# Waits of a fused attention and mixture kernel, set at other points

## The reference

```python
def attn(data, weight, mask):                       # 32x32 block mask
    block_mask = mask.reshape(nb, 32, kb, 32).sum(axis=(1, 3)) > 0
    elem_mask = repeat(repeat(block_mask, 32, 0), 32, 1)
    return einsum('bsk,nk->bsn', data, weight * elem_mask)

def ffn(x, W_base, b_base, W_router, A, B):         # 8 experts, rank 16, top 2
    probs = softmax(x @ W_router.T); combine = normalised top-2 weights
    h = einsum('nd,erd->ner', x, A)
    expert_out = einsum('ner,eor->no', h * combine[:, :, None], B) * 2.0
    return x @ W_base.T + b_base + expert_out

x = x + attn(layernorm(x), weight, mask)            # x: (2, 4096, 4096) float32
x = x + ffn(layernorm(x), W_base, b_base, W_router, A, B)
```

## Time and profile before

| | |
|---|---|
| median of 3 runs | 1446.66 us (1446.52 to 1446.85) |
| profiled execution | 1448.56 us |
| its span, slowest core | 1446.9 us |
| spans of the cores | 1428.7 to 1446.9 us |
| PE busy | 1012.2 us (70%) |
| DVE busy | 518.3 us (36%) |
| moved by DMA | 179.69 MB |

### The profile page before, as it was taken

The page is one execution under the profiler, slowest core; times in us unless marked ns, Lnnn a source line. Parts: engine busy times, 40 slices in busy tenths (PEclk is TensorE's granted clock), DMA queues, the critical chain, the costliest instruction groups (busy, mean ns, idle before and its releaser), DMA issues.

```text
span 1446.9 us, 19848 instructions; the slowest of 8 cores (1428.7 to 1446.9 us)
## 1 busy us (share of the span) xinstructions
PE 1012.2 (70%) x8874; PEld 854.6 (59%) x8874; DVE 518.3 (36%) x656; ACT 9.7 (1%) x26; POOL 32.2 (2%) x48
## 2 busy tenths in 40 slices
PE   0000000002599999999999806499999999999997
PEld 0000000000488888888888703388888888888886
DVE  2446888662435455445536143400001000000010
ACT  0000000000000000000000000000000000000000
POOL 0000000000000000000000000000000000000000
PEclk9999999999999999999999957699999999999999
DMA  8999989961533533533443089434444555544441
GB/s 207 270 260 236 298 250 285 287 230 28 91 59 71 106 59 60 100 76 59 81 96 60 9 163 162 75 72 104 88 88 88 98 110 117 114 88 88 88 95 53
DMA packets 107887, 179.69 MB, mean 124 GB/s; under 512 B 68234, under 2 KB 84762, under 8 KB 103706
## 3 DMA queue, kind: packets, MB, share of 16 engines
q0 software_dynamic: 19792, 77.67, 30.0%
q1 hardware_dynamic: 85578, 67.17, 17.0%
q10 hardware_dynamic: 2432, 33.57, 6.7%
HBM read 222.48 MB, written 16.78 MB: 165 GB/s over the span
## 4 chain that ended last, share of the span: by engine, by line
PE 67%; DMA 17%; DVE 10%; SPq 4%; issue 2%; DVEq 0%; ACT 0%; POOL 0%; POOLq 0%; ACTq 0%
PE pp L620 32%; PE pp L380 31%; DMA xres<-x_in 10%; DVE ost L220 4%; SPq L148 4%; DMA wts<-mask_in 3%; PE pp L635 2%; DMA packed<-bmt_sb 2%; PE pp L629 2%; DVE scr L251 2%; DMA wts<-wta 1%; DVE wts L335 1%; DMA xnt<-ost 1%; DMA r<-bp_l 1%; DVE bnall L413 0%
## 5 line engine op out<-in xcount | busy, mean ns | idle before, releaser
L380 PE MATMUL pp<-wts,xnt 128*128 128x256 bf16 x4096 | 448.9, 273 | 26.5 <-DVE wts L335 26.5
L620 PE MATMUL pp<-wts,xnt 128*128 128x256 bf16 x4096 | 460.9, 276 | 0.0
L380 PEld LDWEIGHTS pp<-wts,xnt 128*128 128x128 bf16 x4096 | 401.5, 98 | 73.8 <-issue 26.7
L620 PEld LDWEIGHTS pp<-wts,xnt 128*128 128x128 bf16 x4096 | 405.0, 99 | 53.7 <-issue 0.4
L232 PE MATMUL pp<-ost,bd_sb 128*4 128x128 bf16 x32 | 8.5, 265 | 291.8 <-DVE ost L220 291.8
L651 DVE TENSOR_TENSOR ost<-pp,xres 128x256 f32<-128x256 f32 x128 | 43.9, 416 | 469.0 <-PE pp L635 469.0
L335 DVE TENSOR_TENSOR wts<-wts,r 128x8192 bf16<-128x8192 bf16 x16 | 139.1, 8693 | 159.1 <-DMA wts<-wta 159.1
L232 PEld LDWEIGHTS pp<-ost,bd_sb 128*4 128x4 bf16 x32 | 2.6, 80 | 293.7 <-issue 293.7
L220 DVE TENSOR_REDUCE ost<-wts 128x128 bf16<-128x4096 int32 x32 | 141.4, 4420 | 90.3 <-DMA wts<-mask_in 87.1
L348 DVE TENSOR_TENSOR xres<-pp,xres 128x256 bf16<-128x256 f32 x128 | 43.9, 415 | 101.2 <-PE pp L380 101.2
L465 PE MATMUL pp<-wrt,xnt 128*128 128x8 bf16 x256 | 7.7, 167 | 48.9 <-DMA xnt<-xstg 35.0
(11 more groups left out here) (51 smaller groups left out, 133.3 us busy)
## 6 DMA issues: line engine op xcount, KB each, us to landing
wts<-mask_in ACTq DMA_DIRECT2D x16, 2048.0 KB, 10.3
wts<-mask_in SPq DMA_DIRECT2D x16, 2048.0 KB, 11.3
wts<-wta POOLq DMA_DIRECT2D x16, 2048.0 KB, 14.7
wts<-wtb POOLq DMA_DIRECT2D x16, 2048.0 KB, 16.8
y_out<-ost SPq DMA_DIRECT2D x16, 1024.0 KB, 16.1
xres<-x_in POOLq DMA_DIRECT2D x8, 1024.0 KB, 19.7
r<-at_l POOLq DMA_DIRECT2D x1, 1024.0 KB, 7.9
r<-bp_l POOLq DMA_DIRECT2D x1, 1024.0 KB, 7.8
```

The costliest lines, as they stand in the source:

```text
L380: f = (lambda t, kt=kt, tt=tt, b=b, bank=bank, c0=c0, st=st: t.matmul(bank[:, c0:c0 + slab_n], xnt[:, tt, kt, :], wts[:, b, kt, :], start= ...
L620: top(lambda t, kt=kt, tt=tt, b=b, bank=bank: t.matmul(bank[:, 256 * (tt % 2):256 * (tt % 2) + slab_n], xnt[:, tt, kt, :], wts[:, b, kt, : ...
```

## The change

The first transpose of the first layer norm no longer waits for the loads of all x tiles. The weight loads of attention's slabs 0 and 1 wait for the last mask reduction that reads the buffer in question, where all loads waited for the whole mask and all transposes; the multiplication by the mask (slabs 0 and 1) waits for the mask, and the first matmul for the transposes. The loads of at, bp and bias wait only for the last multiplication by the mask, and no longer for each other; the first transpose of the second layer norm does not wait for them.

```diff
--- before.py
+++ after.py
@@ -257,8 +257,6 @@
             if i >= 13 and (i - 13) % 2 == 0 and (i - 13) // 2 < n_tt:
                 tt = (i - 13) // 2
                 w = [(pV, ln1_ap[tt])]
-                if tt == 0:
-                    w.append((sXc, c_xcast_all))
                 ln1_xb[tt] = xbar((sB0 if tt % 2 == 0 else sB1),
                                   xnt[:, tt, :, :], ln1_src(tt), waits=w)
             if i >= 11 and (i - 11) % 2 == 0 and (i - 11) // 2 < n_tt:
@@ -330,7 +328,9 @@
         def emit_attn_apply(s):
             b = s % 2
             w = [((sW0 if b == 0 else sW1), c_wcast[s])]
-            if s >= 2:
+            if s < 2:
+                w.append((pV, v_mask_done))
+            else:
                 w.append((pT, t_slab[s - 2]))
             return vop(lambda v, b=b, s=s: v.tensor_tensor(
                 wts[:, b].rearrange("p a (j r) -> p a j r", r=32),
@@ -356,11 +356,12 @@
         v_applies = []
         for s in range(n_slab):
             b = s % 2
-            w = [(sB0, ln1_b0), (sB1, ln1_b1), (pV, v_mask_done)]
-            if debug and s < 2:
-                w.append((sAt, dbg_pre_attn))
-            if s >= 2:
-                w.append((pT, t_slab[s - 2]))
+            if s < 2:
+                w = [(pV, v_red[n_mtile - 2 + s])]
+                if debug:
+                    w.append((sAt, dbg_pre_attn))
+            else:
+                w = [(pT, t_slab[s - 2])]
             c_wcast.append(dma(RG, (sW0 if b == 0 else sW1),
                                wts[:, b, :, :].rearrange("p a c -> p (a c)"),
                                wta[s], waits=w, max_dma_last_dim=8192))
@@ -368,6 +369,9 @@
             if s >= 1:
                 pass
             w = [(pV, v_applies[s])]
+            if s == 0:
+                w.append((sB0, ln1_b0))
+                w.append((sB1, ln1_b1))
             if s >= 2:
                 w.append((pV, v_evac[s - 2]))
             first = True
@@ -441,12 +445,9 @@
         ln2_aggr = [None] * n_tt
 
         c_at = dma(RG, sAt, at3.rearrange("p a c -> p (a c)"), at_l[:],
-                   waits=[(pT, t_attn_done), (pV, v_applies[-1])],
-                   max_dma_last_dim=8192)
-        c_bp = dma(RG, sAt, bprime, bp_l[:], waits=[(sAt, c_at)],
-                   max_dma_last_dim=8192)
-        c_bias = dma(RG, sAt, bias_sb[:, :], bias_in,
-                     waits=[(pV, v_mask_done), (sAt, c_bp)])
+                   waits=[(pV, v_applies[-1])], max_dma_last_dim=8192)
+        c_bp = dma(RG, sAt, bprime, bp_l[:], max_dma_last_dim=8192)
+        c_bias = dma(RG, sAt, bias_sb[:, :], bias_in)
 
         tw = min(4, n_tt)
         nth = n_tt // tw
@@ -522,8 +523,6 @@
                 xstg_ln2[pb], xres[:, tt, :], ri_buf[pb][:], nm_buf[pb][:],
                 op0=ALU.mult, op1=ALU.add), waits=wap)
             w = [(pV, ln2_ap[tt]), (pT, t_attn_done)]
-            if tt == 0:
-                w.append((sAt, c_bias))
             ln2_xb[tt] = xbar((sB0 if tt % 2 == 0 else sB1),
                               xnt[:, tt, :, :], xstg_ln2[tt % 2], waits=w)
             emit_router(tt)
```

## The result

The changed kernel takes 0.9862 of the time before (95% interval 0.9832 to 0.9892), about 20 us less; its profiled execution took 1428.27 us, its span is 1426.7 us, and the undisturbed runs lie between 1427.85 and 1430.58 us. The forecast was 1430.5. That ratio has a condition on which much of this study turned: it leaves out the runs in which single cores were far behind, and of the changed kernel's first ten timed runs those are five, with 1455 to 1474 us. The median of all ten is 1442.94 us, against 1447.04 us before. Runs in which the cores of one die were held back together at a lower granted clock (1494 to 1654 us, the kernel before among them) are in no count in this document.

The account below looks back on a forecast made before the run. The slowest core, core 3, was taken to set the time, with gains only outside its unbroken matmul stages; 0 + 7.6 + 8.5 = 16.1 us off 1448.56 gives 1432.4, less 1.9 to the runs' median: 1430.5 us, range 1421 to 1441.

Parts of the forecast that it names:

- part 1: First layer norm: first transpose no longer waits for all x; 0 to 1.9 us on core 3, taken as 1.
- part 2: Before attention: weight loads 0 and 1 go out early; 17.3 us less 9.7 us of slower gathers gives 7.6 us.
- signs of being wrong: Gather steps under 2.1 or over 6 us, mask tiles 28 to 31 over 3 us later, other slowest core, other matmul-stage lengths.
- C: Rival at the gathers: served only after both weight loads, which take longer; slower than before, 1450 us at 36 us; chance 0.04.
- The 17.3 us: Front stretch, core 3: time from last gather's result to first mask multiplication, 352.85 to 370.13, expected to leave the path.
- the gather step beside a load: One step of the gather chain while weight loads fill the engines: taken as 3.0 us, against 1.63 us undisturbed.
- S: Time the gather chain loses to the two early weight loads: 9.7 us, between 0 and 18.1.
- Rival A: Starved gathers before attention: a step of 6 us or more, loss 14 to 21 us, 1439 us; chance 0.20.
- rival B: Cheap gathers before attention: a step waits for one packet at most, 2.05 us; 1425 or 1421 us; chance 0.19.
- Part 3: Between the stages: at, bp and bias load earlier, so second-stage transposes start at 838.7, not 847.2; 8.5 us (7.5 to 8.7).
- The cover: End of attention: the some 18 us of at, bp and bias loads lie beside two slabs of matmuls and cost nothing.
- contention between cores: Mask reading: early weight reads of fast cores delay slow cores' mask tiles; taken as 1 us.

Follow-up runs that it names:

- parts 2 and 3 with load 1 later: Changed kernel with the first transpose's wait kept and weight load 1 waiting for the whole mask: 1427.6 us, ratio 0.9844 to the kernel before.
- the run with the load inside the transpose: Kernel before with only the first transpose's wait removed and the last x load held until mask tile 12 is reduced: 1463 to 1469 us.
- the run of parts 2 and 3: Changed kernel with the first transpose's wait for all x loads kept: 1435.8 us, ratio 0.9914 to the kernel before.
- The experiment with load 1 later: Changed kernel, but weight load 1 waits for the whole mask: two best runs 1421.9 and 1422.0 us, one 1437.6, two of five with a late core.
- the run with smaller pieces: Changed kernel with weight loads 0 and 1 cut into rows of 1024 elements, not 8192: multiplication 46 us behind the cast, not 42.6; no total time given.
- the run of part 2 alone: Kernel before with only the edits to weight loads, mask multiplication and first matmul: ratio 0.9979 (0.9957 to 1.0001), 3 us less.

## Why the prediction was right, and where it was not

The forecast of 1430.5 us lies among the five undisturbed timed runs, 1.2 us over their median. That is luck in part: two errors cancelled, part 1 taken too low and part 2 too high, and about half of the runs are not undisturbed. Two of the prediction's own signs of being wrong showed, a gather step over 6 us (6.67) and a slowest core other than 3 or 6 (core 7).

**Part 1, forecast 0 to 1.9 us (taken as 1): wrong, on both sides.** The step that failed is "A transpose that goes out 4.9 us earlier and takes 3 to 9 us longer brings tile 14 no earlier", and with it the choice of core 3 of one profile as the core that decides. In the profile after, the transpose took 8.69 us on the slowest core, DVE began tile 14 at 161.32 and not 167.49, and the mask ended 7.0 us earlier.

Not all of the 7.0 is part 1, since these are two single executions: the normalised tile itself was ready at 141.2 on core 7, and at 147.0 on core 3 before. The last core's cast lies at 318.6 to 323.9 us in seven profiles with the wait in place, and at 316.1 to 318.8 in five without it, each time without the cores whose transpose was stretched to 23 us or more; the means are 321.0 and 317.7, some 3 us apart. The times say the same: 3 us alone, and 3.5 to 5.7 us on top of parts 2 and 3 with load 1 later. On the chip of the last set the two undisturbed runs with part 1 (1430.7 and 1439.0) cannot be told from those without it (1429.6 to 1442.8). Which core is late in the mask changes from run to run. In the profile before the wait stands on all cores with 1.5 to 14.6 us, and on core 3, which I had picked, with 4.9; that it is part of the slowest core's time in most runs, also where one profile shows it short, is my reading.

On the other side, I bounded the stretched transpose by 14.28 us, the longest row beside mask loads. Beside an x load it reached 39.25 us, and in 19 of 36 runs a core lay 25 to 53 us behind the median of the eight. No rival named this loss: C, the one on the slower side, had another place. That the missing wait is the cause rests on the count (19 of 36 against none of 78) and on the two stretched transposes caught, both with an x load issued inside them. What remains open is why it strikes on one core and not on its neighbour with the same overlap: the run with the load inside the transpose has both. Without part 1 a transpose beside two mask loads once took 23.68 us (core 0 of the run of parts 2 and 3), and that run took 1442.8 us; so the mask loads alone have a milder form of it.

**Part 2, forecast 7.6 us: mechanism right, size off.** The 17.3 us left the path, and the gathers paid. The mis-sized term is the gather step beside a load: taken as 3.0 us, measured 5.1 to 6.7 on core 7 (up to 7.1 on the other cores). The four long steps take 20.2 us in all (21.2 forecast). From the cast to the last gather's result it is 42.4 us (316.05 to 358.44) and was 29.8 (323.02 to 352.85), so S is 12.6 us, where I had 9.7. That leaves 4.5 us between the marks and 3 us for the part alone.

The other term, 17.3 us, held only where load 0 is long. Before, it kept the multiplication waiting for 16.5 to 17.0 us on cores 1, 3, 4 and 6, which needed 47.1 to 48.5 us from the cast to the multiplication, and for 12.8 to 13.6 us on the other four, which needed 43.0 to 44.2. After, all eight need 42.2 to 43.8. So where load 0 was short, the gathers took back nearly all that the part gave.

The experiment with load 1 later shows the cause: with one load beside them, one step is long (5.69 us). Rival A's step ("6 us or more") was nearer than my own; rival B's step of 2.05 us or less is refuted. I had read the rule of the Trainium skill (DMA: Bandwidth & Descriptors, "Queues, rings and completion order") as one packet of the profile for a turn, 0.42 us; the steps grew by 3.5 to 5 us. That page of the Trainium skill speaks of packets of about 9 to 17 descriptors, and if each of the profile's packets is one descriptor, that is an estimate of 3.8 to 7.1 us, which fits. But the run with smaller pieces does not bear it out as a count of pieces: they were about an eighth of the size, and the step did not move. The mask loads of other cores, for which I had taken 1 us, were not visibly delayed by early weight reads (casts at 309.1 to 318.6 us in the run of part 2 alone, 306.7 to 323.0 before).

**Part 3, forecast 8.5 us: right.** 8.1 us between the marks and 8.4 alone. The cover I named, two slabs of matmuls, is needed: with the loads issued at the transposes the kernel took 13 us more, not the "nothing" that was true only of the idle DMA engines at 800 to 820.

**The sum.** Forecast 0 + 7.6 + 8.5 (with 1 us of part 1 and 1 us of contention between cores against each other); measured 7.0 + 4.5 + 8.1 between the marks. Parts 2 and 3 alone multiply to 0.9921, together 0.9914: they add up, within the intervals. The 2.9 us (0.2%) that I took for the reach of a measurement came from three runs that lay close together; the kernel before later ran from 1446.1 to 1458.2 us.

## What to carry to other kernels

A wait that looks needless may keep two transfers apart that had better not meet: before taking it away, list what will be in the DMA engines together, and look at all runs of the new kernel and all its cores, not at the best ones. A load that is moved forward out of the critical chain can land on small DMAs that are in it, and what it gives is then only its own length less what they lose; then move only what is needed first (load 0), and put the small ones in flight together, so that their delay is paid once. Where the slowest core changes from run to run, a gain must be weighed over all cores, since one profile shows one draw.

## What the runs showed of the hardware

A DMA transpose of 1 MB (5.0 us alone) took 6 to 14 us beside mask loads, 23.7 once; 13 to 23 us beside two cast loads from POOL; and up to 39.25 us beside a cast load and mask loads, while the engines were counted busy and moved 53 to 108 GB/s for 20 us of it. The Trainium skill (DMA: Bandwidth & Descriptors, "Rules for kernel authors") says that a transpose next to ordinary DMAs needs nothing; it speaks there of intact data, and these runs show that the time is another matter.

A 1 KB DMA within SBUF took 1.6 us with the DMA engines idle, 5.1 to 6.0 us beside one weight load (the first step on the eight cores of the run with load 1 later), and 5 to 7 us beside two, whatever the size of their pieces (19792 or 26960 packets in the ring). Chained gathers paid it three to four times, gathers in flight together once.
